# Query remainder on 64 contraction rows in the unmasked attentions of a graph and attention kernel

## The chip, the cores and the metric

One core of one Trainium2 chip runs the whole program in one launch. The metric is the device time of a launch in microseconds.

## The reference

`x` has 1250 rows (nodes or tokens) of 512 float32 values. First a two-layer graph network on 41250 edges is added to it. Then a block with three attentions in a row follows, 8 heads of 64 each; the router picks one of four experts for the first two:

```python
h = h + gnn(layernorm(x), edges)
xn, xt = ln(x, s), ln(x, t)
spatial = mha(xn, expert_s)                      # unmasked
temporal = xt + mha(xt, expert_t, causal=True)   # masked
fused = mha(q=spatial, kv=temporal)              # unmasked
x = x + fused
x = x + gelu(ln(x) @ w1.T + b1) @ w2.T + b2
# mha: softmax(q k^T) v per head, T = 1250 queries and keys, head size 64
```

All of it is in float32.

## The kernel before

Products run in a reduced-precision float32 format (fp32r), so each factor is split into a high part and a remainder, and the partial products are added in PSUM. Tokens go in 10 blocks of 125 (`P = 125`, `NT = 10`). A head has 64 values, so 128 contraction rows hold two things at once: `QSH[b]` holds the high part of the head's queries twice, in rows 0 to 63 and again in 64 to 127; `QSL[b]` holds the queries' remainder twice; `KS[b]` holds the keys' high part in rows 0 to 63 and their remainder in rows 64 to 127. `b` is the head's parity. One product of `QSH` with `KS` over 128 rows gives high x high and high x remainder; one of `QSL` with `KS` gives remainder x high and remainder x remainder.

`load_heads` (SyncE, L441) loads `QSL` and `KS` of a head as soon as the scores of the head before last are done. `cut_heads` (GpSimd, L649) splits them: `QSH` from `QSL` (L583), then in four pieces of up to 314 keys the high part of rows 64 to 127 into a scratch `KT` (L661) and the remainder in place (L664), then the high part of rows 0 to 63 (L583), the queries' remainder (L670), and the values (L679, L682). Each step counts up the semaphore `A.cut`, 13 counts for a head; `scores` waits for count 11 and `values` for 13 of its head. In the same GpSimd stream stand the inverses of the softmax sums (`spread`), weights that are split (L583, L598), and at the end `residual_rows` (L638, L641). SyncE waits for all of `A.cut` before it loads `XR` and `XL`.

An unmasked attention is a loop over `n` = 80 supers (8 heads x 10 query blocks). The order on TensorE is `scores(n+1)`, `turn_probs(n)`, half of `values`:

- `scores(n)` (L943): 1250 keys in three PSUM banks of 512, 512 and 226 columns (`CHUNKS`). For each bank it waits for `A.lo` of super n-2 on that bank, then L966 (`QSH`) and L967 (`QSL`), 125 query columns each as the loaded weights. The last product signals `A.scores`. Supers use two sets of three banks in turn.
- `turn_probs` (L981): ten transposes of the exponentials into the same banks.
- `values` (L1000): ten products of 252 columns for the pair of supers before.
- three times for a pair of heads, except for the last, the inverses are spread over the rows: 8, 8 and 4 products at L1016.

On VectorE the order is `greatest(n+1)` (L1767: the negated maximum over all 1250 scores, after `A.scores`), `probs_lo(n)` (L1776: three pieces, one for a bank, remainder of the transposed probabilities; each signals `A.lo`), and now and then an output (L1793) or a normalisation (L1819). ScalarE takes the high part of the transposed probabilities (L1186), then the exponentials of n+1 (L1173), and now and then the lower half of an output (L1196). L1491 brings the value projection out of PSUM ahead of an attention; `product_tile` (L730 to L732) is the projection behind the last one, which needs the cut remainder of the heads' outputs (VectorE L1460) and the split weights.

The masked attention does 40 supers, each of two query blocks, with the general form of the loop in `scores`.

Of the kernel before, what the change touches and what calls it, by code (L numbers as in the profile page):

```python
# [15 lines left out]
F32 = mybir.dt.float32  # L16
# [3 lines left out]
ALU = mybir.AluOpType  # L20
# [4 lines left out]
T, D, H, HD, NEXP = 1250, 512, 8, 64, 4  # L25
P = 125
# [22 lines left out]
HG = NT // 2  # L49
NQ = 4  # L50
BLOCKS = [(0, 3), (3, 6), (6, NT)]


ORDER = ["g1l", "g1r", "g2l", "g2r", "qs", "ks", "vs", "qo", "qt", "kt", "vt", "ut", "kc", "vc", "uc"]
# [39 lines left out]
class Attn:  # L94
# [3 lines left out]
    def __init__(self, turn, causal):  # L98
        self.turn, self.causal = turn, causal
        self.S = NT // 2 if causal else NT  # L100
        self.N = H * self.S
        self.per = 2 * self.S
        self.ends = self.N + (1 if causal else 0)
        self.G = 3 if causal else HG
        self.W = 12 * 252 if causal else NT * 252
        self.spans = ((0, 3), (3, 4), (7, 4)) if causal else ((0, 2), (2, 4), (6, 4))
        self.runs = [self.runs_of(k) for k in range(self.S)]
        self.cum = [sum(len(r) for r in self.runs[:k]) for k in range(self.S + 1)]
        full, half = H * NT, H * NT // 2
        self.supers0 = (0, full, full + half)[turn]  # L110
        self.groups0 = (0, H * HG, H * HG + H * 3)[turn]
        self.runs0 = 0
        self.cuts0 = 13 * H * turn
        self.qin0 = 32 * H * turn
        self.pairs0 = H // 2 * turn

# [98 lines left out]
def gnn_ffn_program(nc, x, src, dst, weights, qkv_bias, out_bias, row_bias, ln_cols, mlp_b1,  # L215
                    router_w1, router_w2, router_b1, router_b2, out):
    with ExitStack() as ctx:
# [36 lines left out]
        def flat(a):  # L254
            return ps[:, 3 * a:3 * a + 3, :].rearrange("p a b -> p (a b)")
# [86 lines left out]
        KS = [R[:, HB + 5000:HB + 6250], R[:, HB + 6250:HB + 7500]]  # L342
        VS = [R[0:P, HB + 7500 + 1280 * b:HB + 8780 + 1280 * b].rearrange("p (c n) -> p c n", c=NT) for b in range(2)]
        KT = R[:, HB + 10060:HB + 10374]
        K_CUTS = [slice(lo, min(lo + 314, T)) for lo in range(0, T, 314)]
        ident_r = R[0:P, HB + 10374:HB + 10374 + P + 1]
        mask_r = R[0:P, HB + 10500:HB + 10500 + P + 2]
        mask = TB[0:P, 2, 128:128 + P + 2]
# [78 lines left out]
        def _(eng):  # L427
# [104 lines left out]
            eng.wait_ge(pj["qk"].a, 20)  # L532
            load_heads(KT_)
            load_units(UNIT["ut"], 4, e_t * 16 + (T0 + 12))
            eng.wait_ge(A.cut, 26 * H)
            eng.wait_ge(sp["t"].st0, 32)
            eng.wait_ge(sp["t"].st1, 32)
            eng.dma_start(XR, xt_d).then_inc(xr_in, 16)
# [6 lines left out]
            eng.wait_ge(qc_in, 16)  # L545
            load_heads(KC_)
            load_row(4, ROWB["uc"])
            eng.wait_ge(A.cut, 39 * H)
            eng.dma_start(XL[0:P], x1_d.rearrange("i p f -> p i f")).then_inc(xl_in, 16)
            load_units(UNIT["uc"], 4, C0 + 12)  # L550
            load_row(5, ROWB["m2"])
# [10 lines left out]
        def _(eng):  # L562
# [18 lines left out]
            def hi_part(to, a):  # L581

                return eng.tensor_tensor(to, a, zero[0:to.shape[0], :].to_broadcast(list(to.shape)), ALU.add)  # L583
# [46 lines left out]

            def residual_rows():

                eng.wait_ge(A.cut, 39 * H)
                eng.wait_ge(row_in, 16 * 5)
                eng.wait_ge(xl_in, 16)
                for i in range(NT):
                    y = YL[0:P, i, :]
                    eng.tensor_scalar(y, XL[0:P, i, :], mr1[0:P, i, 0:1], mr1[0:P, i, 1:2], ALU.subtract, ALU.mult  # L638
                                      ).then_inc(y_norm, 1)
                    eng.wait_ge(y_norm, i + 1)  # L640
                    eng.tensor_tensor(y, y, brow[0:P, :], ALU.add).then_inc(y_ready, 1)  # L641
                eng.wait_ge(y_ready, NT)
                eng.sem_inc(row_free, 1)
# [5 lines left out]
            def cut_heads(K):  # L649
                for hp in range(H // 2):  # L650
                    for b in range(2):
                        n0 = K.cuts0 + 26 * hp + 13 * b
                        eng.wait_ge((A.qin0, A.qin1)[b], K.qin0 + 64 * hp + 64)
                        eng.sem_inc(held, 1)

                        hi_part(QSH[b], QSL[b].bitcast(F32)).then_inc(A.cut, 1)
                        eng.wait_ge(A.cut, n0 + 1)
                        eng.sem_inc(held, 1)
                        for part, sl in enumerate(K_CUTS):
                            keys, top_ = KS[b][64:128, sl], KT[64:128, 0:sl.stop - sl.start]  # L660
                            eng.tensor_tensor(top_, keys.bitcast(F32), zero[64:128, :].to_broadcast(list(top_.shape)),  # L661
                                              ALU.add).then_inc(A.cut, 1)
                            eng.wait_ge(A.cut, n0 + 2 + 2 * part)
                            eng.tensor_tensor(keys, keys.bitcast(F32), top_.bitcast(F32), ALU.subtract  # L664
                                              ).then_inc(A.cut, 1)
                            eng.wait_ge(A.cut, n0 + 3 + 2 * part)
                            eng.sem_inc(held, 1)
                        hi_part(KS[b][0:64, :], KS[b][0:64, :].bitcast(F32)).then_inc(A.cut, 1)
                        eng.wait_ge(A.cut, n0 + 10)
                        eng.tensor_tensor(QSL[b], QSL[b].bitcast(F32), QSH[b].bitcast(F32), ALU.subtract  # L670
                                          ).then_inc(A.cut, 1)
                        eng.wait_ge(A.cut, n0 + 11)

                        if hp:
                            eng.wait_ge(A.pv, K.group((2 * hp + b - 1) * K.G - 1))
                        eng.sem_inc(held, 1)
                        eng.wait_ge(pj["v"].v, NT * (K.turn + 1))
                        vh = V[0:P, :, 128 * hp + 64 * b:128 * hp + 64 * b + 64]
                        eng.tensor_copy(VS[b][:, :, 0:64], vh).then_inc(A.cut, 1)  # L679
                        eng.wait_ge(A.cut, n0 + 12)  # L680
                        eng.sem_inc(held, 1)
                        eng.tensor_tensor(VS[b][:, :, 64:128], vh, VS[b][:, :, 0:64].bitcast(F32), ALU.subtract  # L682
                                          ).then_inc(A.cut, 1)
                    if hp:
                        if hp == 1:
                            eng.wait_ge(w_used, UNIT[("qo", "ut", "uc")[K.turn]])
                        spread(K, hp - 1)
                u = UNIT[("qo", "ut", "uc")[K.turn]]
                cut_units(u, u + ahead(K))
                if K.turn == 2:  # L690
                    residual_rows()
                eng.wait_ge(A.bc, 3 * (K.pairs0 + H // 2))
# [34 lines left out]
        def _(eng):  # L727
# [215 lines left out]
            def scores(K, n):  # L943

                h, k = divmod(n, K.S)
                if k == 0:
                    eng.wait_ge(A.cut, K.cuts0 + 13 * h + 11)
                free = -1
                b = h % 2
                for i, first, blocks, _ in K.parts(n):  # L950
                    end = first + P * blocks
                    end += end % 2
                    odd = (first + P * i) % 2
                    d0 = first + P * i - odd
                    at = first
                    while at < end:
                        bank = at // BANK
                        to = min(end, BANK * bank + BANK)
                        if bank > free:
                            free = bank  # L960
                            if n >= 2:
                                eng.wait_ge(A.lo, K.run(n - 2, bank))
                        keys = KS[b][:, at - first:to - first]
                        piece = flat(n % 2)[0:P, at:to]
                        diagonal = K.causal and to > d0
                        eng.matmul(piece, QSH[b][:, P * i:P * i + P], keys, start=True, stop=False)  # L966
                        ins = eng.matmul(piece, QSL[b][:, P * i:P * i + P], keys, start=False, stop=not diagonal)  # L967
                        if diagonal:
                            d = max(at, d0)
                            col = d - d0 + 1 - odd  # L970
                            ins = eng.matmul(flat(n % 2)[0:P, d:to], ident_r[:, 0:P], mask_r[:, col:col + to - d],
                                             start=False, stop=True)
                        at = to
                ins.then_inc(A.scores, 1)
# [10 lines left out]
            def values(K, m, lo, hi):  # L985

                h = m // K.G
                if lo == 0:
                    last = 2 * m + 1 if not K.causal else h * K.S + min(2 * (m % 3) + 1, K.S - 1)
                    eng.wait_ge(A.lo, K.run(last, 2))  # L990
                    if m >= 2:
                        eng.wait_ge(A.post, K.group(m - 2))
                    if K.held_by(m) is not None:
                        eng.wait_ge(A.norm, K.held_by(m))
                    if m % K.G == 0:
                        eng.wait_ge(A.cut, K.cuts0 + 13 * h + 13)
                chunks = K.chunks(m)
                for c, offset, to, width, start, stop in chunks[lo:hi]:
                    for p in range(2):
# [1026 lines left out]
```

## Time and profile before

| | |
|---|---|
| time, median of 3 runs | 1731.62 us (1729.8 to 1737.79) |
| profiled execution's own time | 1727.27 us |
| its span | 1725.5 us |
| TensorE matmuls busy | 1596.2 us, 93% |
| VectorE, ScalarE, GpSimd busy | 67%, 51%, 43% |
| granted TensorE clock, mean | 0.974 |

The page gives each engine's busy time, the span in 40 slices and the chain of work that ended last. PE is TensorE, PEld its weight loads, DVE VectorE, ACT ScalarE, POOL GpSimd, SP SyncE. Matmuls are pipelined: a matmul's duration contains the way through the array, so consecutive ones overlap in the rows, and the difference of two starts is the time that one costs. The three attentions lie at about 434 to 734, 852 to 1044 and 1135 to 1433 us.

### The profile page before, as it was taken

How to read it: one execution, taken by the hardware profiler on the slowest of the kernel's cores; microseconds unless marked ns; L12 is line 12 of the kernel's file. 1: busy time of each engine (PE TensorE's matmuls, PEld its weight loads, DVE VectorE, ACT ScalarE, POOL GpSimd, SP SyncE). 2: the span in 40 equal slices, each digit the busy share in tenths (PEclk: the TensorE clock that was granted, in tenths of full speed). 3: DMA queues.
4: the chain of work that ended last, by engine and by line, in shares of the span. 5: the costliest groups of instructions: out<-in, count | busy, mean ns of one | idle time of the engine just before them, and what ended most of it. 6: DMA issues, size and time to landing. Idle time of an engine off the chain costs nothing.

```text
span 1725.5 us, 26353 instructions
## 1 busy us (share of the span) xinstructions
PE 1596.2 (93%) x9714; PEld 1355.3 (79%) x9714; DVE 1148.8 (67%) x1810; ACT 879.1 (51%) x1733; POOL 734.6 (43%) x596
## 2 busy tenths in 40 slices
PE   2788999699999999999999998999999997899997
PEld 1567877588788888878789996878888885678876
DVE  7998826720788988840288885168888887843323
ACT  3795313320788878732177772158878873301100
POOL 3120222145446545033568744363546465532430
PEclk9999999799999999989999998999999998899999
DMA  3000021333111112042222304302111210110111
GB/s 105 13 26 2 26 66 46 111 147 72 23 39 31 31 31 61 2 184 69 60 60 61 73 7 156 85 1 52 40 31 31 55 66 19 37 38 25 49 36 59
DMA packets 37347, 91.62 MB, mean 53 GB/s; under 512 B 6457, under 2 KB 8975, under 8 KB 36712
## 3 DMA queue, kind: packets, MB, share of 16 engines
q1 hardware_dynamic: 37224, 89.99, 18.9%
q8 instruction: 75, 1.23, 0.3%
q14 instruction: 48, 0.39, 0.1%
HBM read 45.40 MB, written 13.86 MB: 34 GB/s over the span
## 4 chain that ended last, share of the span: by engine, by line
PE 78%; DVE 8%; ACT 5%; POOL 4%; issue 3%; DMA 2%; DVEq 1%; SPq 0%; POOLq 0%; ACTq 0%
PE ps L1000 12%; PE ps L730 12%; PE ps L731 11%; PE ps L732 11%; PE ps L981 11%; PE ps L966 7%; PE ps L967 6%; DMA w_raw<-in_weights 1%; PE ps L925 1%; PE ps L926 1%; POOL F L638 1%; PE ps L1016 1%; ACT F L1173 1%; ACT F L1260 1%; DVE F L1568 1%
## 5 line engine op out<-in xcount | busy, mean ns | idle before, releaser
L1186 ACT ACTIVATE R<-ps 125x500 fp32r<-125x500 f32 (+3 forms) x632 | 291.8, 508 | 147.0 <-PE ps L981 145.6
L583 POOL TENSOR_TENSOR w_hi<-w_raw,zero 128x512 fp32r<-128x512 f32 x92 | 110.5, 1201 | 593.0 <-PE ps L732 282.4
L1767 DVE TENSOR_REDUCE TB<-ps 125x1 f32<-125x1250 f32 (+4 forms) x240 | 299.5, 1263 | 82.9 <-PE ps L967 56.5
L1776 DVE TENSOR_TENSOR R<-ps,R 125x500 fp32r<-125x500 f32 (+3 forms) x632 | 324.1, 569 | 12.9 <-ACT R L1186 12.9
L1173 ACT ACTIVATE F<-ps,TB 125x1250 f32<-125x1250 f32 (+4 forms) x240 | 276.1, 1157 | 60.2 <-DVE TB L1767 60.2
L1000 PE MATMUL ps<-R 125*128 125x252 f32 (+1 forms) x2080 | 288.9, 286 | 2.3 <-DVE F L1819 2.3
L981 PE MATMUL ps<-ident,F 125*125 125x125 f32 x2040 | 260.1, 275 | 9.6 <-ACT F L1173 8.5
L1000 PEld LDWEIGHTS ps<-R 125*128 125x128 f32 x2080 | 256.0, 189 | 2.6 <-DVE R L1776 1.6
L981 PEld LDWEIGHTS ps<-ident,F 125*125 125x125 f32 x2040 | 239.8, 189 | 12.9 <-ACT F L1173 12.4
L966 PE MATMUL ps<-R 128*125 128x512 f32 (+5 forms) x624 | 240.5, 386 | 5.1 <-DVE R L1776 4.0
L730 PE MATMUL ps<-R,w_hi 128*128 128x512 f32 (+3 forms) x576 | 212.1, 368 | 24.4 <-POOL w_lo L598 13.9
L967 PE MATMUL ps<-R 128*125 128x512 f32 (+5 forms) x624 | 218.3, 353 | 0.0
L583 POOL TENSOR_TENSOR R<-R,zero 128x1250 fp32r<-128x1250 f32 (+1 forms) x48 | 108.9, 2270 | 254.7 <-DMA R<-F 250.1
L731 PE MATMUL ps<-R,w_lo 128*128 128x512 f32 (+3 forms) x576 | 207.7, 361 | 0.0
L732 PE MATMUL ps<-R,w_hi 128*128 128x512 f32 (+3 forms) x576 | 207.4, 360 | 0.0
L730 PE MATMUL ps<-w_hi,R 128*125 128x512 f32 x440 | 180.0, 409 | 8.4 <-DVE R L1460 6.0
L966 PEld LDWEIGHTS ps<-R 128*125 128x125 f32 x624 | 115.9, 186 | 81.7 <-DVE R L1776 73.9
L731 PE MATMUL ps<-w_hi,R 128*125 128x512 f32 x440 | 175.2, 398 | 0.0
L732 PE MATMUL ps<-w_lo,R 128*125 128x512 f32 x440 | 174.7, 397 | 0.0
L730 PEld LDWEIGHTS ps<-R,w_hi 128*128 128x128 f32 x576 | 111.6, 194 | 43.2 <-POOL w_lo L598 14.4
L1491 DVE TENSOR_TENSOR F<-ps,brow 125x512 f32<-125x512 f32 x40 | 27.4, 692 | 175.2 <-PE ps L732 175.0
L598 POOL TENSOR_TENSOR w_lo<-w_raw,w_hi 128x512 fp32r<-128x512 f32 x92 | 132.2, 1437 | 7.2
(203 smaller groups left out, 2416.2 us busy)
## 6 DMA issues: line engine op xcount, KB each, us to landing
R<-F SPq DMA_DIRECT2D x96, 312.5 KB, 5.2
w_raw<-in_weights SPq DMA_DIRECT2D x88, 256.0 KB, 2.6
F<-in_weights SPq DMA_DIRECT2D x3, 1024.0 KB, 8.5
x_d<-F SPq DMA_DIRECT2D x10, 250.0 KB
zt_d<-F SPq DMA_DIRECT2D x1, 2500.0 KB, 14.0
F<-zt_d SPq DMA_DIRECT2D x1, 2500.0 KB, 9.3
xt_d<-F SPq DMA_DIRECT2D x4, 625.0 KB, 3.1
qc_d<-F SPq DMA_DIRECT2D x4, 625.0 KB, 5.7
```

Of the source, the lines that this page charges most:

```text
L583: return eng.tensor_tensor(to, a, zero[0:to.shape[0], :].to_broadcast(list(to.shape)), ALU.add)
L730: eng.matmul(to, ah, bh, start=first, stop=False)
L731: eng.matmul(to, al, bh, start=False, stop=False)
L732: return eng.matmul(to, ah, bl, start=False, stop=last)
L966: eng.matmul(piece, QSH[b][:, P * i:P * i + P], keys, start=True, stop=False)
L967: ins = eng.matmul(piece, QSL[b][:, P * i:P * i + P], keys, start=False, stop=not diagonal)
L981: ins = eng.transpose(ps[0:P, 3 * (n % 2) + bank, P * (j - j0):P * (j - j0) + P], PW[0:P, n % 2, P * j:P * j + P], ident[0:P, 0:P])
L1000: ins = eng.matmul(ps[:, pair_bank(m), to:to + width], VS[h % 2][:, c, :], probs(K, m, p, offset, width), start=start and p == 0, stop=sto ...
L1173: ins = eng.activation(PW[0:P, n % 2, P * first:P * first + P * blocks], flat(n % 2)[0:P, at:at + P * blocks], ACT.Exp, bias=ngm[0:P, 2 * ...
L1186: eng.activation(probs_run(K, n, 0, part, lo, hi), ps[0:P, 3 * (n % 2) + bank, P * (lo - j0):P * (hi - j0)] .rearrange("p (c t) -> p c t", ...
L1767: ins = eng.tensor_reduce(out=ngm[0:P, 2 * (n % 2) + part:2 * (n % 2) + part + 1], in_=flat(n % 2)[0:P, at:at + P * blocks], op=ALU.max, a ...
L1776: eng.tensor_tensor(probs_run(K, n, 1, part, lo, hi), ps[0:P, 3 * (n % 2) + bank, P * (lo - j0):P * (hi - j0)] .rearrange("p (c t) -> p c ...
```

## The change

In the unmasked attentions `scores` issues, for a super, first the three `QSH` products over 128 rows, with the waits on `A.lo` in front of them, and then the three `QSL` products, each over 64 rows: banks 0 and 2 over rows 0 to 63, bank 1 over rows 64 to 127. So that those rows hold the keys' high part, keys 512 to 1023 lie exchanged in `KS`: the remainder in rows 0 to 63, the high part in rows 64 to 127. The product remainder x remainder is no longer formed. `cut_heads` cuts the keys' remainders in five pieces (256, 256, 226 keys in the upper rows, 256, 256 in the lower ones) and the high parts in three, so a head has 17 counts. This cut is used in all three attentions; the masked one keeps its products.

```diff
+CUTS = 17
@@ cut_heads, views
-        K_CUTS = [slice(lo, min(lo + 314, T)) for lo in range(0, T, 314)]
+        K_CUTS = [(64, slice(0, 256)), (64, slice(256, 512)), (64, slice(1024, T)), (0, slice(512, 768)), (0, slice(768, 1024))]
+        K_HIGH = [(0, slice(0, 512)), (64, slice(512, 1024)), (0, slice(1024, T))]
@@ cut_heads
-                        for part, sl in enumerate(K_CUTS):
-                            keys, top_ = KS[b][64:128, sl], KT[64:128, 0:sl.stop - sl.start]
-                            eng.tensor_tensor(top_, keys.bitcast(F32), zero[64:128, :].to_broadcast(list(top_.shape)),
+                        for part, (half, sl) in enumerate(K_CUTS):
+                            keys, scratch = KS[b][half:half + 64, sl], KT[half:half + 64, 0:sl.stop - sl.start]
+                            eng.tensor_tensor(scratch, keys.bitcast(F32),
+                                              zero[half:half + 64, :].to_broadcast(list(scratch.shape)),
                                               ALU.add).then_inc(A.cut, 1)
...
-                        hi_part(KS[b][0:64, :], KS[b][0:64, :].bitcast(F32)).then_inc(A.cut, 1)
-                        eng.wait_ge(A.cut, n0 + 10)
+                        for half, sl in K_HIGH:
+                            keys = KS[b][half:half + 64, sl]
+                            eng.tensor_tensor(keys, keys.bitcast(F32),
+                                              zero[half:half + 64, :].to_broadcast(list(keys.shape)), ALU.add
+                                              ).then_inc(A.cut, 1)
+                        eng.wait_ge(A.cut, n0 + 14)
@@ scores
-                    eng.wait_ge(A.cut, K.cuts0 + 13 * h + 11)
+                    eng.wait_ge(A.cut, K.cuts0 + CUTS * h + 15)
                 free = -1
                 b = h % 2
+                if not K.causal:
+                    cols = slice(P * k, P * k + P)
+                    for bank, (lo, count) in enumerate(CHUNKS):
+                        if n >= 2:
+                            eng.wait_ge(A.lo, K.run(n - 2, bank))
+                        eng.matmul(flat(n % 2)[0:P, lo:lo + count], QSH[b][:, cols], KS[b][:, lo:lo + count],
+                                   start=True, stop=False)
+                    for bank, (lo, count) in enumerate(CHUNKS):
+                        half = 64 * (bank % 2)
+                        ins = eng.matmul(flat(n % 2)[0:P, lo:lo + count], QSL[b][half:half + 64, cols],
+                                         KS[b][half:half + 64, lo:lo + count], start=False, stop=True)
+                    ins.then_inc(A.scores, 1)
+                    return
```

The other waits on `A.cut` (in `values`, `residual_rows` and SyncE's loads of `XR` and `XL`) have their constants multiplied to match.

## Rows read from the trace of the kernel before

**Rows 1.** The page: engines' busy time, the span in 40 slices, the chain's shares.

```profile
PE 1596.2 (93%) x9714; PEld 1355.3 (79%) x9714; DVE 1148.8 (67%) x1810; ACT 879.1 (51%) x1733; POOL 734.6 (43%) x596
...
PE ps L1000 12%; PE ps L730 12%; PE ps L731 11%; PE ps L732 11%; PE ps L981 11%; PE ps L966 7%; PE ps L967 6%; DMA w_raw<-in_weights 1%; PE ps L925 1%; PE ps L926 1%; POOL F L638 1%; PE ps L1016 1%; ACT F L1173 1%; ACT F L1260 1%; DVE F L1568 1%
```

**Rows 2.** Chain in order of time, 608.5 to 620: start, us, what.

```profile
by line: PE ps L1000 34.8%; PE ps L981 33.3%; PE ps L966 17.7%; PE ps L967 15.0%
...
611.46 1.10 PE ps L981 x10
```

**Rows 3.** TensorE's timeline, 611 to 615: start us, us, engine, line, form, count.

```profile
611.29 1.26 PE L981 MATMUL ps<-ident,F 125*125 125x125 f32 x10
612.31 1.42 PE L1000 MATMUL ps<-R 125*128 125x252 f32 x10
613.56 0.40 PE L966 MATMUL ps<-R 128*125 128x512 f32 x1
613.79 0.40 PE L967 MATMUL ps<-R 128*125 128x512 f32 x1
...
614.50 0.37 PE L966 MATMUL ps<-R 128*125 128x226 f32 x1
614.71 0.27 PE L967 MATMUL ps<-R 128*125 128x226 f32 x1
614.82 1.26 PE L981 MATMUL ps<-ident,F 125*125 125x125 f32 x10
```

**Rows 4.** Weight loads, 613.9 to 614.8; in brackets idle time before and its releaser.

```profile
613.92 0.18 PEld L966 LDWEIGHTS ps<-R 128*125 128x125 f32 x1 [0.17 <-DVE R L1776]
614.50 0.18 PEld L966 LDWEIGHTS ps<-R 128*125 128x125 f32 x1 [0.28 <-DVE R L1776]
614.61 0.19 PEld L967 LDWEIGHTS ps<-R 128*125 128x125 f32 x1
```

**Rows 5.** VectorE's timeline, 611.4 to 614.5.

```profile
611.49 1.46 DVE L1767 TENSOR_REDUCE TB<-ps 125x1 f32<-125x1250 f32 x1 [0.57 <-PE ps L967]
612.87 1.58 DVE L1776 TENSOR_TENSOR R<-ps,R 125x250 fp32r<-125x250 f32 x3
```

**Rows 6.** TensorE's timeline, 567.3 to 568.7, the end of a spread super.

```profile
568.44 0.27 PE L966 MATMUL ps<-R 128*125 128x226 f32 x1
568.55 0.27 PE L967 MATMUL ps<-R 128*125 128x226 f32 x1
```

**Rows 7.** Groups by line and form, TensorE, whole span: busy us, mean ns.

```profile
L966 PE MATMUL ps<-R 128*125 128x226 f32 x168 | 59.2, 352 | 0.1
```

**Rows 8.** Waits, 433 to 735: waiter, releaser: us in total, times, longest.

```profile
PEld ps L966 <- DVE R L1776: 32.4, 139, 0.6
```

**Rows 9.** GpSimd's timeline, cuts of the first two heads, first attention.

```profile
425.08 2.27 POOL L583 TENSOR_TENSOR R<-R,zero 64x1250 fp32r<-64x1250 f32 x1 [0.18 <-POOL R L664]
427.42 2.87 POOL L670 TENSOR_TENSOR R<-R 128x1250 fp32r<-128x1250 f32 x1
...
439.09 0.71 POOL L661 TENSOR_TENSOR R<-R,zero 64x314 fp32r<-64x314 f32 x1 [0.18 <-POOL R L583]
```

**Rows 10.** TensorE's timeline, the first score product of the first attention.

```profile
433.73 0.47 PE L966 MATMUL ps<-R 128*125 128x512 f32 x1 [0.30 <-DVE F L1491]
```

**Rows 11.** TensorE's timeline, 1440 to 1447, first products after the last attention.

```profile
1440.64 0.76 PE L730 MATMUL ps<-w_hi,R 128*125 128x512 f32 x1 [0.60 <-DVE R L1460]
...
1443.09 0.76 PE L730 MATMUL ps<-w_hi,R 128*125 128x512 f32 x1 [0.83 <-DVE R L1460]
...
1446.34 0.79 PE L730 MATMUL ps<-w_hi,R 128*125 128x512 f32 x1 [1.63 <-POOL w_lo L598]
```

**Rows 12.** GpSimd's timeline in the same stretch.

```profile
1443.92 2.36 POOL L598 TENSOR_TENSOR w_lo<-w_raw,w_hi 128x512 fp32r<-128x512 f32 x1
```

More of the change, by code:

```diff
@@ L112, in __init__ @@
         self.runs0 = 0
-        self.cuts0 = 13 * H * turn
+        self.cuts0 = CUTS * H * turn
         self.qin0 = 32 * H * turn
@@ L534, in _ @@
             load_units(UNIT["ut"], 4, e_t * 16 + (T0 + 12))
-            eng.wait_ge(A.cut, 26 * H)
+            eng.wait_ge(A.cut, 2 * CUTS * H)
             eng.wait_ge(sp["t"].st0, 32)
@@ L547, in _ @@
             load_row(4, ROWB["uc"])
-            eng.wait_ge(A.cut, 39 * H)
+            eng.wait_ge(A.cut, 3 * CUTS * H)
             eng.dma_start(XL[0:P], x1_d.rearrange("i p f -> p i f")).then_inc(xl_in, 16)
@@ L631, in residual_rows @@
             def residual_rows():
-                eng.wait_ge(A.cut, 39 * H)
+                eng.wait_ge(A.cut, 3 * CUTS * H)
                 eng.wait_ge(row_in, 16 * 5)
@@ L651, in cut_heads @@
                     for b in range(2):
-                        n0 = K.cuts0 + 26 * hp + 13 * b
+                        n0 = K.cuts0 + CUTS * (2 * hp + b)
                         eng.wait_ge((A.qin0, A.qin1)[b], K.qin0 + 64 * hp + 64)
@@ L658, in cut_heads @@
                         eng.sem_inc(held, 1)
-                        for part, sl in enumerate(K_CUTS):
-                            keys, top_ = KS[b][64:128, sl], KT[64:128, 0:sl.stop - sl.start]
-                            eng.tensor_tensor(top_, keys.bitcast(F32), zero[64:128, :].to_broadcast(list(top_.shape)),
+                        for part, (half, sl) in enumerate(K_CUTS):
+                            keys, scratch = KS[b][half:half + 64, sl], KT[half:half + 64, 0:sl.stop - sl.start]
+                            eng.tensor_tensor(scratch, keys.bitcast(F32),
+                                              zero[half:half + 64, :].to_broadcast(list(scratch.shape)),
                                               ALU.add).then_inc(A.cut, 1)
                             eng.wait_ge(A.cut, n0 + 2 + 2 * part)
-                            eng.tensor_tensor(keys, keys.bitcast(F32), top_.bitcast(F32), ALU.subtract
+                            eng.tensor_tensor(keys, keys.bitcast(F32), scratch.bitcast(F32), ALU.subtract
                                               ).then_inc(A.cut, 1)
@@ L667, in cut_heads @@
                             eng.sem_inc(held, 1)
-                        hi_part(KS[b][0:64, :], KS[b][0:64, :].bitcast(F32)).then_inc(A.cut, 1)
-                        eng.wait_ge(A.cut, n0 + 10)
+                        for half, sl in K_HIGH:
[4 more added lines that the diff above has]
+                        eng.wait_ge(A.cut, n0 + 14)
                         eng.tensor_tensor(QSL[b], QSL[b].bitcast(F32), QSH[b].bitcast(F32), ALU.subtract
                                           ).then_inc(A.cut, 1)
-                        eng.wait_ge(A.cut, n0 + 11)
+                        eng.wait_ge(A.cut, n0 + 15)
                         if hp:
@@ L679, in cut_heads @@
                         eng.tensor_copy(VS[b][:, :, 0:64], vh).then_inc(A.cut, 1)
-                        eng.wait_ge(A.cut, n0 + 12)
+                        eng.wait_ge(A.cut, n0 + 16)
                         eng.sem_inc(held, 1)
@@ L995, in values @@
                     if m % K.G == 0:
-                        eng.wait_ge(A.cut, K.cuts0 + 13 * h + 13)
+                        eng.wait_ge(A.cut, K.cuts0 + CUTS * h + CUTS)
                 chunks = K.chunks(m)
```

## The prediction

> **What bounds the kernel now.** I read the page first: TensorE is busy for 93% of the span, VectorE for 67%, and lines L966 and L967 (the two products of `scores`) hold 13% of the chain that ended last [rows 1]. A busy TensorE is a share and not yet a reason, so the next view is order in time inside one unmasked attention, where the change is. There the chain goes wholly through TensorE: ten L981 transposes, ten L1000 products, six score products, in turn [rows 2]. That looks like an engine that would gain from any column taken away. The timeline says otherwise at one place. The four score products of 512 columns follow one another at 0.23 to 0.24 us, which is their streaming time. But the third bank's first product (226 columns, 614.50) stands 0.21 us ahead of its partner (614.71), has a duration of 0.37 us, and the partner stands only 0.11 us ahead of the transposes [rows 3]. The weight load rows explain it: the load for this product starts at 614.50, after 0.28 us of idle time released by VectorE L1776, and the matmul can stream only when that load is in, 0.11 us later. The second bank's load at 613.92 is held in the same way, 0.17 us [rows 4]. L1776 is `probs_lo`: `scores(n)` may overwrite a PSUM bank only after `probs_lo(n-2)` has read it. VectorE is where the held time comes from: the reduction of `greatest` starts at 611.49 and takes 1.46 us, three L1776 pieces follow without a gap (a merged row of 1.58 us from 612.87) and end at 614.45 [rows 5].
>
> So a super (one block of 125 query rows) is a closed loop. Call T the first transpose after the scores (611.29). Reduction starts at T + 0.20; it and the three pieces end at T + 3.16; the load of bank 2 goes at T + 3.21; the hi product streams 0.11 later, T + 3.32, the lo product at T + 3.42, and the next T is T + 3.53 (614.82) [rows 3 to 5]. Each term is a row, and the sum is the period. TensorE's own work (1.02 us of transposes and 1.25 us of values bring it to T + 2.27, then 0.94 us of the first four score products) reaches T + 3.21 as well [rows 3]: the two limits tie, and either alone gives about the same period. An attention has supers where the loop is slack: those in which the inverses are spread (L1016, eight extra matmuls). There the third bank's product has duration 0.27 us and spacing 0.11 [rows 6]. Over the whole trace the 168 products of this form average 352 ns [rows 7]; between 270 (free) and 370 (held) that makes (352 - 270) / 100 x 168 = 138 held ones. In the first attention alone loads of L966 are held by L1776 139 times, two for a held super, which agrees [rows 8].
>
> **The change part by part.** First, the order of the six products. Before: bank 0 hi, lo, bank 1 hi, lo, bank 2 hi, lo. After: hi of banks 0, 1, 2, then lo of 0, 1, 2. The waits for L1776 stay at the hi products. Behind the last wait there now stand one hi product of 226 columns and *all three* lo products, where before one of each stood. That is work moved from under the wait to behind it. Behind the weight load of bank 2 (0.11) come: before 0.11 + 0.11 (weight load at 614.61, transposes at 614.82) [rows 3, 4], after 0.11 (hi 2) + the lo products. The reduction of the next super waits for the last of them, and everything on VectorE hangs on that.
>
> Second, the lo products contract over 64 rows: lo 0 and lo 2 in rows 0 to 63, lo 1 in rows 64 to 127. Nothing in the kernel orders lo 0 against lo 1 (other rows, other banks). The trace has no such pair. Bounds: wholly at the same time, or one after the other at 0.235 us each [rows 3]. Side by side lo 0 and lo 1 take 0.235, lo 2 0.11. So a held super grows by 0.235 (side by side) or 0.47 (one after the other). I take side by side, since the operands share neither rows nor banks and weight loads and matmuls of this trace overlap in just this way [rows 4]. By the Trainium skill (TensorE: Matmul & The Clock Gate, Part 3, The mechanism) matmuls in different row groups do run at the same time; no run here shows it yet.
>
> Third, a switch between products over all rows and products over half of them, twice a super. Its lower bound is nothing; a gain is excluded, since no load can be drawn ahead of a held load. Upper bound: the matmul waits for the end of the one before and then loads its weights. The end lies 0.27 - 0.11 = 0.16 us behind the next start of a free 226-column product [rows 6], the load costs 0.11 [rows 4], together 0.27. I take 0.16, the row nearest to two neighbours that must not overlap; both ends stay in the range. By the Trainium skill (TensorEngine Tiling (Array Packing), Key Properties) "changing tiling mode (not just tile) drains the TensorE": by that rule the 0.16 is due, without it the switch is free and the first rival below holds. This rule speaks against the change. The first switch lies on the loop. The second (before the transposes) lies beside VectorE's reduction: TensorE comes to bank 1 0.23 us early and to bank 2 0.34 us early in the new order (2.27 + 0.235 against 2.63 + 0.11; then 2.98 against 3.32), so up to 0.23 costs nothing in a held super.
>
> Fourth, spread supers. There are 3 for each of 3 head pairs in 2 unmasked attentions, 18. There TensorE's sum decides [rows 6], so they gain 0.235 and pay both switches. In the 6 short ones (four L1016 matmuls, 0.45 us) TensorE asks for bank 2 at T + 3.19 and the wait to T + 3.21 returns with its load, so the gain is about 0.08. Together -(12 x 0.235 + 6 x 0.08) = -3.3 us.
>
> Fifth, GpSimd's `cut_heads`: four instructions more for a head (17 semaphore counts for 13), the same elements. From 0.71 us for 314 columns and 2.27 for 1250 an instruction has a fixed 0.19 us; four are 0.75, two more waits 0.18 each [rows 9], in all 1.1 us a head, in all 24 heads. Before the first head of the first attention the keys and queries are cut at 427.42 + 2.87 = 430.29, and scores start at 433.73, held by L1491 (3.4 us of cover); the pattern and the cover are the same in all three attentions [rows 9, 10]. Within an attention the cuts run a head ahead: zero. In the tail GpSimd is on the path: the last cut starts when its DMA lands, then x1 and four weight units are loaded, rows normalised, and the last unit is cut at 1446.3, where TensorE waits for it; VectorE's own chain would have let it start some 0.8 to 1.0 us earlier (the spacing of the two starts before, 2.45 from 1443.09, gives 1445.5) [rows 11, 12]. The 1.1 us moves that end to 1447.4; the last two heads, slower by 20 x 0.235 = 4.7, overtake it, so of those 4.7 us about 1.0 is hidden. SyncE's two waits on `A.cut` (for XR and XL) only have new constants. The masked attention keeps its products; keys 512 to 1023 with parts exchanged give the same sums.
>
> **The sum.** Held supers 138 x 0.235 = +32.4; spread supers -3.3; tail -1.0: +28.1 us with a free switch. Switch at 0.16: 138 x 0.16 = 22.1, and 18 x 0.32 = 5.8: +27.9. Together +56.0 on the profiled execution's own 1727.3 us (span 1725.5 and 1.8 around it), 1783.3. That execution lies 4.3 us under the median of the runs shown (1731.6), so the median comes to 1787.6; the cases below are counted from that median too.
>
> **The rivals.**
> Free switch: side by side and nothing for the change of shape. +28.1, 1759.7. For it: nothing in the kernel's own rows shows a drain. Against it: a load can't be drawn under the hi product of other rows if the array is one piece.
> No overlap: the 64-row products run one after the other, so the change doesn't do what it says. Held supers +0.47, spread ones nothing: 64.9 - 1.0 = +64, 1796 with a free switch; with 0.16, 64 + 28 = +92, 1823. For it: no row of before shows two matmuls streaming at once.
> TensorE's columns decide: if L1776's ends aren't what holds bank 2, 512 fewer columns in 156 supers save 0.235 each: -37 us, 1695, faster than before. It turns on one point: the new order must find bank 2 free at T + 2.74 (where TensorE gets there), not T + 3.21. For it: the chain that ended last names TensorE alone [rows 2]. Against it: the held loads and the 0.37 to 0.27 us contrast. With switches of 0.12 each the same case is level: 156 x (0.24 - 0.235) = 0; with 0.16 each it is +13, 1745.
>
> **How the numbers follow.** Side by side with a paid switch 0.42; free switch 0.24; no overlap 0.22 (0.08 free, 0.14 paid); TensorE's columns 0.12. The likeliest gives 1787.6; its own range, switch from 0.08 to 0.27, is 1774 to 1807 (at 0.27: 138 x 0.27 + 18 x 0.54 = 47, so +75; at 0.08 half of 27.9, so +42). The range that leaves out no more than 2 in 10 goes from the free switch, less 6 for the count of held supers, to no overlap with 0.16: 1754 to 1824. Faster by over 0.5% 0.07, within 0.5% 0.04, slower by over 0.5% 0.89 (about half a percent is what a measurement of this kernel can tell from no change).
>
> **What would show each step.** The period from transpose to transpose in a plain super: 3.53 before; 3.93 by the forecast, 3.77 with a free switch, 4.0 without overlap, 3.3 if columns decide. The load of the hi product of bank 2 should still start within 0.05 us of the third L1776 piece, with bank 0's and bank 1's hi products both done well ahead. Starts of lo 0 and lo 1 within 0.11 us of each other show the overlap; lo 0 0.27 us instead of 0.11 behind hi 2 shows the switch. VectorE's idle time before L1767 should grow by as much as the period, TensorE's idle or stretched time should sit before hi 1 and hi 2, and L1767, L1776, L981 and L1000 should keep their durations. The masked attention should keep its 22 us a head, and no score product should wait for L670. The forecast is wrong if bank 2 is free before TensorE asks for it, or if lo 0's start shows no price and no partner.

## The result, and the profile after

The changed kernel takes 1791.68 us (median of four runs, 1790.6 to 1794.78) against 1730.71 us for the kernel before (four runs, 1727.53 to 1737.79): ratio 1.0351, 95% interval 1.0327 to 1.0374. The forecast was 1787.6. The profiled span is 1788.6 us, 63.1 more than the 1725.5 of before.

The page of the changed kernel, busy times of the engines, and the chain that ended last by engine and by line:

```profile
PE 1648.6 (92%) x9714; PEld 1357.2 (76%) x9714; DVE 1148.4 (64%) x1810; ACT 879.3 (49%) x1733; POOL 747.9 (42%) x692
...
PE 56%; DVE 31%; ACT 5%; issue 3%; POOL 3%; DMA 2%; SPq 0%; DVEq 0%; POOLq 0%; ACTq 0%
DVE R L1796 12%; DVE TB L1787 11%; PE ps L737 11%; PE ps L738 10%; PE ps L739 10%; PE ps L966 5%; PE ps L962 4%; PE ps L1001 4%; PE ps L1020 3%; PE ps L1036 1%; PE ps L932 1%; DVE R L1480 1%; PE ps L933 1%; PE ps L986 1%; ACT F L1280 1%
```

VectorE does the same work (1148.4 us against 1148.8) and is yet 31% of the chain, where it was 8% on the page of before. `probs_lo` (L1796 here, L1776 before) and `greatest` (L1787, was L1767) stand first; transposes and values (L1001, L1020, were L981 and L1000, 23% in [rows 1]) have dropped to 7%. The chain in order of time from 620 to 632, of which one super is shown (start us, us, what):

```profile
by line: DVE R L1796 42.5%; DVE TB L1787 36.5%; PE ps L966 13.5%; PE ps L962 9.2%; issue 1.7%
...
621.77 1.46 DVE TB L1787
623.23 1.51 DVE R L1796 x3
624.73 0.04 issue
624.78 0.37 PE ps L962
625.15 0.55 PE ps L966 x2
625.69 0.02 issue
625.71 1.46 DVE TB L1787
```

This is the loop of the prediction, spelled out by the profile itself: maximum, three pieces, the hi product of bank 2, the lo products, the next maximum, 3.94 us from 621.77 to 625.71. In [rows 2] the same view named TensorE alone. The two limits lay close together before; now the loop stands alone.

TensorE's timeline, its weight loads and VectorE's timeline in the same super. L962 are the hi products over 128 rows ("hi" is high part of the queries, "lo" their remainder; hi 0 is bank 0's), L966 the lo products over 64 rows; brackets hold idle time and its releaser:

```profile
621.66 1.35 PE L1001 MATMUL ps<-ident,F 125*125 125x125 f32 x10
622.77 1.41 PE L1020 MATMUL ps<-R 125*128 125x252 f32 x10
624.02 0.39 PE L962 MATMUL ps<-R 128*125 128x512 f32 x1
...
624.78 0.37 PE L962 MATMUL ps<-R 128*125 128x226 f32 x1
625.08 0.50 PE L966 MATMUL ps<-R 64*125 64x512 f32 x2
...
625.41 0.26 PE L966 MATMUL ps<-R 64*125 64x226 f32 x1
625.61 1.35 PE L1001 MATMUL ps<-ident,F 125*125 125x125 f32 x10
```

```profile
624.78 0.18 PEld L962 LDWEIGHTS ps<-R 128*125 128x125 f32 x1 [0.40 <-DVE R L1796]
625.07 0.29 PEld L966 LDWEIGHTS ps<-R 64*125 64x125 f32 x3
625.61 1.17 PEld L1001 LDWEIGHTS ps<-ident,F 125*125 125x125 f32 x10 [0.24 <-issue]
```

```profile
621.77 1.46 DVE L1787 TENSOR_REDUCE TB<-ps 125x1 f32<-125x1250 f32 x1 [0.67 <-PE ps L966]
623.14 1.58 DVE L1796 TENSOR_TENSOR R<-ps,R 125x250 fp32r<-125x250 f32 x3
```

Read against [rows 3] and [rows 4]: the load for bank 2's hi product starts 0.06 us behind the end of L1796 (623.14 + 1.58 = 624.72), as it started 0.05 behind it before. From there to the last lo product it is 0.63 us (624.78 to 625.41) instead of 0.21 (614.50 to 614.71), and these 0.42 us are the whole growth of the period. They have two parts. From the start of bank 2's hi product to the first 64-row one it is 0.30 instead of 0.21: the loads wait until 625.07, while before the next load went in 0.11 behind. And lo 0 to lo 2 is 0.33: the two 512-column products take 0.50 us together, in a group whose mean is 497 ns for one:

```profile
L966 PE MATMUL ps<-R 64*125 64x512 f32 x320 | 80.0, 497 | 0.0
```

Two products of 497 ns each within 0.50 us can only lie on each other: lo 0 and lo 1 run side by side. The 0.33 is one weight load that nothing hides (0.11, as in the 0.37 us rows of [rows 3]) and one stream of 0.22. A switch (a change between products over 128 and over 64 rows) therefore costs about 0.08 of waiting and a load of 0.11 that is laid bare, 0.19 together.

By stage, from the first score product of an attention (433.73 and 1134.59 before; 434.06 and 1169.71 after) to the first product of the last pair's inverses (731.14 and 1430.75; 764.53 and 1496.35), the first attention grew by 33.1 us (297.4 to 330.5) and the third by 30.5 (296.2 to 326.6). What lies before the first and between the two grew by 0.3 and 1.7, and what follows the third shrank by 2.5; together 63.1.

Not all of the first attention's growth is the loop. Supers are counted from 0 to 79; from super 5 on, the 67 plain ones of each attention (those without the inverses) grew by 0.417 us on average, 27.9 us together. But from the first attention's first score product to the transposes behind the scores of super 4 it is 20.95 us where it was 16.98, and three plain supers at 0.42 explain only 1.25 of these 3.97. The granted clock there was at its lower level (1.2 GHz, 0.50 of full) for 13.6 us (439.3 to 452.9), and before for 3.3 us (439.1 to 442.4); in both TensorE had been busy for half of the 5 us ahead of the fall (2.57 of 5.10, 2.44 of 5.20). In the third attention it stayed at full speed. About 2.7 us of the growth are this stretch. Each is one profiled execution, so how much of it belongs to the change isn't shown.

### The profile page after: what moved, and what is told of

Read it like the earlier page. It is cut to its first block, busy times and chain, and to the rows that moved or that the text cites. A ratio compares the mean times of both kernels' runs of the same rounds, so it can differ in the third digit from the quotient of the medians.

```text
span 1788.6 us, 26473 instructions
## 1 busy us (share of the span) xinstructions
PE 1648.6 (92%) x9714; PEld 1357.2 (76%) x9714; DVE 1148.4 (64%) x1810; ACT 879.3 (49%) x1733; POOL 747.9 (42%) x692
## 4 chain that ended last, share of the span: by engine, by line
PE 56%; DVE 31%; ACT 5%; issue 3%; POOL 3%; DMA 2%; SPq 0%; DVEq 0%; POOLq 0%; ACTq 0%
DVE R L1796 12%; DVE TB L1787 11%; PE ps L737 11%; PE ps L738 10%; PE ps L739 10%; PE ps L966 5%; PE ps L962 4%; PE ps L1001 4%; PE ps L1020 3%; PE ps L1036 1%; PE ps L932 1%; DVE R L1480 1%; PE ps L933 1%; PE ps L986 1%; ACT F L1280 1%
## 5 line engine op out<-in xcount | busy, mean ns | idle before, releaser
L1206 ACT ACTIVATE R<-ps 125x500 fp32r<-125x500 f32 (+3 forms) x632 | 292.2, 508 | 211.2 <-PE ps L1001 209.9
L1787 DVE TENSOR_REDUCE TB<-ps 125x1 f32<-125x1250 f32 (+4 forms) x240 | 299.4, 1262 | 143.1 <-PE ps L966 120.1
L1796 DVE TENSOR_TENSOR R<-ps,R 125x500 fp32r<-125x500 f32 (+3 forms) x632 | 324.4, 569 | 14.4 <-ACT R L1206 14.4
L1020 PE MATMUL ps<-R 125*128 125x252 f32 (+1 forms) x2080 | 289.3, 286 | 2.3 <-DVE F L1839 2.3
L1001 PE MATMUL ps<-ident,F 125*125 125x125 f32 x2040 | 277.3, 284 | 9.1 <-ACT F L1193 8.2
L1001 PEld LDWEIGHTS ps<-ident,F 125*125 125x125 f32 x2040 | 241.0, 190 | 49.8 <-issue 37.6
L1020 PEld LDWEIGHTS ps<-R 125*128 125x128 f32 x2080 | 256.3, 189 | 2.6 <-DVE R L1796 1.6
L962 PE MATMUL ps<-R 128*125 128x512 f32 (+1 forms) x480 | 163.0, 399 | 14.3 <-DVE R L1796 1.0
L585 POOL TENSOR_TENSOR R<-R,zero 128x1250 fp32r<-128x1250 f32 x24 | 54.5, 2273 | 279.3 <-DMA R<-F 279.3
L962 PEld LDWEIGHTS ps<-R 128*125 128x125 f32 x480 | 87.7, 186 | 75.6 <-DVE R L1796 59.5
L738 PEld LDWEIGHTS ps<-R,w_lo 128*128 128x128 f32 x576 | 112.0, 195 | 16.1
```

Of the source, the lines that this page charges most:

```text
L738: eng.matmul(to, al, bh, start=False, stop=False)
L962: eng.matmul(flat(n % 2)[0:P, lo:lo + count], QSH[b][:, cols], KS[b][:, lo:lo + count], start=True, stop=False)
L1001: ins = eng.transpose(ps[0:P, 3 * (n % 2) + bank, P * (j - j0):P * (j - j0) + P], PW[0:P, n % 2, P * j:P * j + P], ident[0:P, 0:P])
L1020: ins = eng.matmul(ps[:, pair_bank(m), to:to + width], VS[h % 2][:, c, :], probs(K, m, p, offset, width), start=start and p == 0, stop=sto ...
L1206: eng.activation(probs_run(K, n, 0, part, lo, hi), ps[0:P, 3 * (n % 2) + bank, P * (lo - j0):P * (hi - j0)] .rearrange("p (c t) -> p c t", ...
L1787: ins = eng.tensor_reduce(out=ngm[0:P, 2 * (n % 2) + part:2 * (n % 2) + part + 1], in_=flat(n % 2)[0:P, at:at + P * blocks], op=ALU.max, a ...
```

## The experiments

The theory: a super's period is the loop through VectorE, so what counts is the work behind the wait for bank 2; 64-row products of two banks run side by side; a switch of shape costs 0.19 us. Rivals: the longer split on GpSimd; TensorE's own sum as the bound, with switches of 0.32 us that make up the 0.41; 64-row products that don't overlap. Each ratio is to the kernel before on the same chip. TensorE's own sum is what a super would take if no product had to wait.

**e1, the split alone.** After's `cut_heads` and counts, and `scores` of before.

```diff
-                if not K.causal:
-                    cols = slice(P * k, P * k + P)
...
-                    return
```

> The new split of keys alone (17 counts a head, keys 512 to 1023 exchanged), with the six score products of before in their old order over 128 rows; the result is the same sum. Loop theory (what stands behind the wait for bank 2 sets the period): period in a plain super 3.53 us as before, total 0 to +1.5 us, the latter from the masked attention. Rival (GpSimd's longer cut, 1.1 us in each of 24 heads, is what costs): a good part of the +61 us is here.

Measured: 1732.69 against 1730.21 us, ratio 1.0013 (1.0001 to 1.0026). Plain supers keep 3.53 us. GpSimd is not the cause. The cost of 2.5 us is a little above the 1.5 expected. A part of it can be seen: in the masked attention one score product of the trace is late for the split (TensorE waits 0.8 us for L677, the cut of the queries' remainder, once), the same wait as in the changed kernel. The prediction had said that none would. TensorE's waits in the masked attention of the changed kernel (waiter, releaser: us in total, times, longest):

```profile
PE ps L986 <- POOL R L677: 0.7, 1, 0.7
```

**e2, the order alone.** All lo products over 128 rows, order hi, hi, hi, lo, lo, lo.

```diff
-                        half = 64 * (bank % 2)
-                        ins = eng.matmul(flat(n % 2)[0:P, lo:lo + count], QSL[b][half:half + 64, cols],
-                                         KS[b][half:half + 64, lo:lo + count], start=False, stop=True)
+                        ins = eng.matmul(flat(n % 2)[0:P, lo:lo + count], QSL[b][:, cols],
+                                         KS[b][:, lo:lo + count], start=False, stop=True)
```

> The changed kernel, but the three lo products over all 128 rows: new order, no 64-row product, no switch, as many columns as before. Loop theory: 0.235 x 2 more work behind the wait, period 3.53 + 0.47 = 4.00 us, total 147 x 0.47 - 2.5 = +66, about 1797 us. Rival (TensorE's sum is the bound, and two switches of 0.32 us each make it slower): no switches and the same columns, so the period stays 3.53 and the total that of before.

Measured: 1794.62 against 1730.21 us, ratio 1.0370 (1.0347 to 1.0394). TensorE's timeline, two supers:

```profile
622.52 0.74 PE L965 MATMUL ps<-R 128*125 128x512 f32 x3
623.09 1.26 PE L1000 MATMUL ps<-ident,F 125*125 125x125 f32 x10
...
626.51 0.74 PE L965 MATMUL ps<-R 128*125 128x512 f32 x3
627.09 1.15 PE L1000 MATMUL ps<-ident,F 125*125 125x125 f32 x9
```

The period is 3.99 to 4.00 us (622.52 to 626.51, and 623.09 to 627.09), with not one column more or less than before and no 64-row product in it. Were TensorE's sum the bound, a mere change of order would have left 3.53. The order alone costs +64 us; 64 rows on top of it take 0.05 us off a plain super (3.99 to 3.94). The medians differ by 3 us (1794.6 and 1791.7), which is within their intervals.

**e3, one 64-row product.** The order of before; only bank 2's lo product, without remainder x remainder, is on 64 rows.

```diff
-                        ins = eng.matmul(piece, QSL[b][:, P * i:P * i + P], keys, start=False, stop=not diagonal)
+                        rows = 64 if bank == 2 and not K.causal else 128
+                        ins = eng.matmul(piece, QSL[b][0:rows, P * i:P * i + P], keys[0:rows, :], start=False,
+                                         stop=not diagonal)
```

> The kernel before, but the lo product of bank 2 contracts over rows 0 to 63 only (it leaves out remainder x remainder for those keys): no new order, no partner, only a switch before and after it. Loop theory with a switch of 0.19 us on the loop and the second one hidden beside VectorE: hi 2 to lo 2 0.30 instead of 0.11, period 3.72 us, total 147 x 0.19 + 18 x 0.39 - 2 = +33, about 1764 us. If TensorE's sum were the bound with 0.32 a switch: period 4.17, +100 us. If 64 rows are free of any switch: no change.

Measured: 1770.58 against 1730.21 us, ratio 1.0226 (1.0202 to 1.0249); period 3.79 us, not 3.72. TensorE's timeline and one row of its weight loads:

```profile
624.52 0.27 PE L966 MATMUL ps<-R 128*125 128x226 f32 x1
624.72 0.36 PE L968 MATMUL ps<-R 64*125 64x226 f32 x1
625.01 1.35 PE L983 MATMUL ps<-ident,F 125*125 125x125 f32 x10
```

```profile
624.72 0.18 PEld L968 LDWEIGHTS ps<-R 64*125 64x125 f32 x1 [0.19 <-issue]
```

Here bank 2's hi product is the free form, 0.27 us long: nothing holds it any more. The load of the 64-row product starts 0.20 us behind that start, the load of the transposes 0.29 later still, each 0.11 ahead of its stream, where two 128-row products stand 0.11 apart and need no bare load. That is 0.20 and 0.18, 0.19 for each switch, two in a super: TensorE's own sum is 3.42 (e5) + 0.38 = 3.80, above the loop (3.53 + 0.19 = 3.72). I had hidden the second switch beside VectorE; with the order of before there is no slack there to hide it. The price of a switch stands, and that of 0.32 falls, which would have given 4.17.

**e4, no partner.** Changed order and 64-row products, but keys laid out and cut as before and all three lo products in rows 0 to 63. In `scores` of the changed kernel:

```diff
-                        half = 64 * (bank % 2)
+                        half = 0
```

> The new order with 64-row lo products, but all three in rows 0 to 63, keys laid out and cut as before: same switches, no partner possible. If banks 0 and 1 ran side by side in the changed kernel (each at its full rate): lo 0 to lo 2 0.47 instead of 0.33 less the 0.11 of the first weight load seen in it, that is about 0.58, period 3.94 + 0.24 = 4.18 us, total about 1791 + 35 = 1826 us. If they ran one after the other anyway and the 0.33 is something else: as the changed kernel, 1791.

Measured: 1833.41 against 1730.21 us, ratio 1.0597 (1.0569 to 1.0624). TensorE's timeline:

```profile
622.34 0.37 PE L955 MATMUL ps<-R 128*125 128x226 f32 x1
622.64 0.83 PE L959 MATMUL ps<-R 64*125 64x512 f32 x3
623.40 0.37 PE L994 MATMUL ps<-ident,F 125*125 125x125 f32 x1
```

The group of three takes 0.83 us instead of 0.60, hi to lo is 0.30 as in the changed kernel, and the period is 4.18 us (622.64 to 626.82). So the exchange of the keys' parts buys 0.24 us a super, one whole 512-column stream: the overlap is complete. By the Trainium skill (TensorE: Matmul & The Clock Gate, Part 3, The mechanism) matmuls in different row groups run at the same time; these runs agree. The whole kernel is 42 us slower than the changed one where 35 were expected; in this trace the granted clock was 0.50 for 17 us at the start of the first attention (from 441.4).

**e5 and e6, a shorter maximum.** If VectorE's 1.46 us lies on the loop, a shorter one must move the period. In the first attention alone the softmax shift is taken from the first 512 keys. Softmax doesn't change with its shift, but the exponentials can overflow for other inputs, so this is a probe and no general kernel. Same edit on the kernel before (e5) and on the changed one (e6):

```diff
-                                                in_=flat(n % 2)[0:P, at:at + P * blocks], op=ALU.max, axis=AX.X,
+                                                in_=flat(n % 2)[0:P, at:at + (P * blocks if K.turn else BANK)],
+                                                op=ALU.max, axis=AX.X,
```

> The kernel before, but in the first attention alone the shift of the softmax is the maximum over the first 512 keys instead of 1250 (the exponentials' shift alone differs; it takes 0.77 us from each reduction on VectorE). Loop theory: bank 2 is then free before TensorE asks, what is left is TensorE's own sum, and the period of the first attention falls from 3.53 to 3.42 us; about 70 supers x 0.11 = -8 us, 1722. Rival (TensorE's sum alone set the period before): 3.53 and no change.

Measured: 1721.35 against 1731.61 us, ratio 0.9938 (0.9921 to 0.9956). TensorE's timeline:

```profile
624.68 0.27 PE L966 MATMUL ps<-R 128*125 128x226 f32 x1
624.78 0.27 PE L967 MATMUL ps<-R 128*125 128x226 f32 x1
624.89 1.26 PE L981 MATMUL ps<-ident,F 125*125 125x125 f32 x10
...
628.10 0.27 PE L966 MATMUL ps<-R 128*125 128x226 f32 x1
```

The held 0.37 us form is gone, and the period is 3.42 us (624.68 to 628.10), TensorE's own sum. From super 5 on, the attention is 7.6 us shorter, as the loop theory says; 1.9 more come from its first supers, where the clock stayed at full speed in this trace.

> The changed kernel with the same shorter maximum in the first attention. Loop theory: bank 2 is free early, the period falls from 3.94 to TensorE's own sum with two switches of 0.19: 3.42 - 0.235 + 0.39 = 3.58 us; about 75 x 0.36 = -27 us against the changed kernel, some 1765, in the first attention only. The third attention keeps 3.94. Rival (switches of 0.32 and TensorE's sum explain the 3.94): the period stays at 3.94.

Measured: 1778.19 against 1731.61 us, ratio 1.0275 (1.0243 to 1.0307). The period falls from 3.94 to 3.73 us, not to 3.58. Weight loads, then VectorE:

```profile
626.31 0.18 PEld L962 LDWEIGHTS ps<-R 128*125 128x125 f32 x1 [0.34 <-DVE R L1797]
```

```profile
624.41 0.42 DVE L1797 TENSOR_TENSOR R<-ps,R 125x250 fp32r<-125x250 f32 x1 [0.19 <-ACT R L1206]
625.00 1.26 DVE L1797 TENSOR_TENSOR R<-ps,R 125x500 fp32r<-125x500 f32 x2 [0.17 <-ACT R L1206]
```

Bank 2 is still asked for early and held. Behind the maximum's loop lies a second one: transposes, ScalarE's high parts (L1206), `probs_lo`, bank 2, lo products. Its first two pieces now wait for ScalarE, not for the maximum. From the transposes at 623.41 it is 0.58 to L1206 (623.99), 1.01 to the second stretch of pieces (625.00), 1.26 for these, 0.05 to bank 2's load (626.31) and 0.83 from there to the next transposes (627.14): 3.73, the period. I had not worked it out. It doesn't help the rival, under which nothing would have moved.

**e7, the pair ahead of the wait.** Order hi 0, hi 1, lo 0 beside lo 1 on 64 rows, wait for bank 2, hi 2 and lo 2 over all rows. `product(q, bank, half, rows)` is one score product; its definition and the loop over hi 0 and hi 1 with their waits are left out:

```diff
...
+                    for bank in range(2):
+                        product(QSL, bank, 64 * bank, 64)
+                    if n >= 2:
+                        eng.wait_ge(A.lo, K.run(n - 2, 2))
+                    product(QSH, 2)
+                    product(QSL, 2).then_inc(A.scores, 1)
```

> The changed kernel's keys, but the order hi 0, hi 1, lo 0 beside lo 1 on 64 rows, then the wait for bank 2, hi 2 and lo 2 over all rows: the overlap is kept and lies ahead of the last wait, both switches lie on TensorE. Loop theory with 0.19 a switch: hi 1 streams at T + 2.74, the pair at 3.17, hi 2 at 3.59, next T at 3.81; period 3.81 us, total about +44, 1774. If a switch cost nothing off the loop: period 3.53 and the time of before. If the new order had nothing to do with it: 3.94 and the changed kernel's time.

Measured: 1770.57 against 1731.61 us, ratio 1.0227 (1.0209 to 1.0245), period 3.79 us (623.75 to 627.54 in the transposes' starts). Weight loads:

```profile
626.37 0.18 PEld L962 LDWEIGHTS ps<-R 128*125 128x125 f32 x1 [0.29 <-DVE R L1802]
626.79 0.18 PEld L962 LDWEIGHTS ps<-R 64*125 64x125 f32 x2 [0.24 <-issue]
627.22 0.29 PEld L962 LDWEIGHTS ps<-R 128*125 128x125 f32 x2 [0.25 <-issue]
```

This is the best place found for the pair, 21 us better than the change, and still 39 us slower than before. Two loads start at once at 626.79, the overlap is there, no VectorE release stands in front of bank 2, and both switches show as idle time of the loads with no releaser. But the loop has not gone: it now closes at bank 1, whose load at 626.37 is held for 0.29 us by `probs_lo` (L1802). Behind that wait stand hi 1, a switch, the pair, a switch, hi 2 and lo 2, and this sum gives the 3.8 that was expected. TensorE's own sum would be 3.42 - 0.235 + 0.38 = 3.57, an estimate that no run reaches; even that is above the 3.53 of before. One stream of 0.235 saved doesn't pay for two switches of 0.19.

## Why the prediction was right, point by point

**The bound.** Right. That supers are held by bank 2, read from the 0.37 against 0.27 us forms of one product and the idle time of its load, is borne out by e2 (order alone), by e5 (held form gone, 3.42 us) and by the chain after. That the two limits lie close was right as well, but they didn't quite tie: e5 gives 3.42 when the loop is loosened, 0.11 under the loop's 3.53.

**The order.** Right: +0.47 forecast for the two streams behind the wait, 0.46 measured (e2).

**The overlap.** Right and whole: e4 against the changed kernel, 4.18 - 3.94 = 0.24 for 0.235.

**The switch.** The next product does wait for the one before; the size was a little low, 0.19 for 0.16. In e3 the 64-row product streams at 624.83 (its load at 624.72 and 0.11), 0.04 us behind the end that its row gives for the product before (624.52 + 0.27 = 624.79); that end is modelled. I had let the product stream at that very end. Its load goes in 0.07 ahead of the end and is bare all the same, so the upper bound, which put the whole load behind the end, was too high. That the choice between the two bounds came so near the measured price was in part luck. By the Trainium skill (TensorEngine Tiling (Array Packing), Key Properties) a change of tiling mode drains TensorE; e3, in which nothing else is changed, agrees so far as these rows show it.

**Held supers.** The count was right. L962's loads wait for L1796 147 times in the changed trace, but that counts banks 0 and 1 as well; of bank 2's loads 139 are held. (The 147 stands in the expectations of e2 and e3 as if it were supers; 140 supers with a wait are plain, 78 in each attention less 8 with inverses.) 140 x 0.417 = 58.4 for my 138 x 0.395 = 54.5, so 3.9 of the sum's miss is here, 3.0 of it from the size of the switch.

**The miss of the sum.** The span grew by 63.1 and the median by 61.0 for the 56.0 forecast. Of the 7.1 us of the span, 3.9 are the plain supers, 2.7 the lower clock at the start of the first attention, which the forecast had no term for, and 2.0 (0.3 + 1.7) lie ahead of the first attention and between it and the third; the spread supers gave 0.3 back and the tail 1.5. That leaves 0.3 unplaced.

**Spread supers.** Transposes to transposes 4.43 us (581.70 to 586.13) for 4.31 before, +0.12; I had -0.235 + 0.32 = +0.09 in the long ones. In the short ones it is 3.98 for 3.85, +0.13, where I had -0.08 + 0.32 = +0.24. I had counted 18; only 16 have scores, since the third pair's last inverses come behind the last scores. In sum +2.2 for +2.5.

**GpSimd.** Zero forecast but for the tail; e1 puts it at +0.13%, with one 0.8 us wait in the masked attention that I had excluded. It is not at the attention's first head, for which I had shown the cover, but at a later one (974.7 us in the changed trace), for which I had only claimed it.

**The tail.** -2.5 us for -1.0. The last unit of weights is now ready ahead of time, and TensorE takes it 1.41 us behind the unit before (1508.54 to 1509.95), where it was 3.25 [rows 11]. I had taken VectorE's spacing of before (2.45) for the next start, but its last piece was done earlier: the same instruction (L1480, was L1460) took 1.45 us from 1508.32, with GpSimd done at 1507.07, and 2.29 us before, beside GpSimd's L598 [rows 12]. The shorter spacing (3.25 to 1.41) is 1.8 of the 2.5 us; where the rest lies isn't shown.

**The second switch.** Hidden in the changed kernel, as said, because there TensorE comes early to bank 2. In e3 I used it where it doesn't hold.

## What to carry to other kernels

When a chain names one engine, look for the one instruction of a repeated group that is longer than its twin. Its waiting weight load can show a loop through another engine that ties with it, and then only the work behind that wait counts, not the engine's columns. Grouping products by kind (all hi, then all lo) moves work behind the last wait, which cost 3.7% here without a column more. Packing two half-height products side by side saves one stream but needs two changes of shape, so it pays only where several streams are saved between two changes, here more than 0.38 us. No run here saved more than one stream, so the point where it pays is an estimate. And look at each bank's wait: moving the pair ahead of the last wait (e7) made the wait before it the one that counts.

## What the runs showed of the hardware that I had not expected

The price of a change between 128-row and 64-row products is 0.19 us each way at a granted clock of 1.00 (2.4 GHz). The next weights aren't loaded under the earlier product's stream as they are between two 128-row products: in e3 and e7 the load idles with no releaser (0.19 to 0.25 us), starts 0.07 ahead of the earlier product's modelled end (e3), and then its 0.11 us is bare. Two 64-row products in different rows have their weights loaded at the same time (x2 at 626.79 within 0.18 us in e7), and e4 against the changed kernel shows that the second one's 512 columns cost nothing beside the first (0.24 us saved of a stream of 0.235).
